# Expert products in float32r halves, and attention with scores one step ahead of the attended sums

## What is computed

```python
# attention, per sequence of 114 rows
xn = layernorm(h)
qk = silu(xn @ wqk + bqk);  q = qk*gamma[0]+beta[0];  k = qk*gamma[1]+beta[1]
v  = silu(xn @ wv + bv)
s  = q @ k.T / 114 + relative_bias          # causal
a  = laplacian(s)                           # (1 + erf(...)) / 2
h  = h + a @ v
# experts, per row: top 2 of 8
xn = layernorm(h)
w, e = softmax over the two largest of xn @ w_router.T
y  = sum_k w_k * ((silu(xn @ w_gate[e_k].T) * (xn @ w_up[e_k].T)) @ w_down[e_k].T)
out = h + layernorm(y) * ln_gamma + ln_beta
```

## Time and profile before

| | |
|---|---|
| runs | median 1163.66 us (1160.97 to 1164.1, 3 runs) |
| profiled execution | 1162.72 us, its span 1160.9 us |
| TensorE busy over the span | 1019.3 us (88%), mean granted clock 0.929 |
| VectorE, ScalarE, GpSimd busy | 714.1, 578.9, 601.2 us |
| chain that ended last, by engine | TensorE 71%, VectorE 7%, GpSimd 5%, DMA 5%, ScalarE 5% |

### The profile page before, as it was taken

How to read it: one execution, slowest core, us unless ns; L and a number is a source line. 1 busy time by engine, 2 the same in 40 slices (tenths; PEclk the granted TensorE clock), 3 DMA queues, 4 the chain that set the end, 5 groups by cost and what they waited for, 6 DMA issues and landing times.

```text
span 1160.9 us, 19799 instructions
## 1 busy us (share of the span) xinstructions
PE 1019.3 (88%) x5646; PEld 818.8 (71%) x5647; DVE 714.1 (62%) x1864; ACT 578.9 (50%) x1273; POOL 601.2 (52%) x662
## 2 busy tenths in 40 slices
PE   5888999999999999998898862999999999999920
PEld 3678999999999999997576641566666666666610
DVE  1666999999999998886666652233333333333337
ACT  1466777877787777664766740222222222222223
POOL 4533776677667767777356565133333333333346
PEclk8998999999999999998978865999999999999965
DMA  9460001000100000120475323122222222222263
GB/s 272 125 182 18 1 1 65 1 1 2 65 1 1 25 1 2 59 61 23 125 283 168 116 60 111 28 45 45 42 45 45 45 45 45 42 45 45 41 151 121
DMA packets 54733, 75.49 MB, mean 65 GB/s; under 512 B 9348, under 2 KB 46978, under 8 KB 52612
## 3 DMA queue, kind: packets, MB, share of 16 engines
q1 hardware_dynamic: 32680, 49.24, 13.5%
q0 software_dynamic: 16640, 18.53, 9.5%
q10 hardware_dynamic: 5340, 6.83, 2.1%
HBM read 45.38 MB, written 29.14 MB: 64 GB/s over the span
## 4 chain that ended last, share of the span: by engine, by line
PE 71%; DVE 7%; POOL 5%; DMA 5%; ACT 5%; issue 5%; SPq 2%; POOLq 0%; ACTq 0%; DVEq 0%
PE bank L1512 19%; PE bank L1224 15%; PE bank L1528 9%; PE bank L1289 7%; PE bank L1284 3%; PE bank L1520 2%; PE bank L1355 2%; PE bank L1367 2%; DMA xtok<-in_tok_emb,tokens_s 2%; PE bank L1272 2%; PE bank L1273 1%; SPq L515 1%; POOL xtok L1002 1%; PE bank L1503 1%; DVE arena_b L1684 1%
## 5 line engine op out<-in xcount | busy, mean ns | idle before, releaser
L1152 POOL DMA_INDIRECT yrows<-arena_b,dest_i x64 | 99.7, 1557 | 273.4 <-ACT arena_b L961 262.2
L1512 PE MATMUL bank<-arena_a,arena_b 128*128 x512 | 236.2, 604 | 0.8 <-ACT arena_b L949 0.6
L1684 DVE SCALAR_TENSOR_TENSOR arena_b<-bank,sml,arena_b 128x304 f32<-128x304 f32 (+2 forms) x384 | 195.3, 522 | 20.0 <-ACT arena_b L742 17.1
L1998 DVE TENSOR_TENSOR arena_b<-bank,arena_b 128x512 f32<-128x512 f32 x64 | 44.3, 692 | 203.0 <-PE bank L1512 203.0
L1512 PEld LDWEIGHTS bank<-arena_a,arena_b 128*128 128x128 f32 x512 | 93.2, 192 | 100.0 <-issue 99.8
L1224 PE MATMUL bank<-xt_hi,w_hi 128*128 128x308 f32 x512 | 159.6, 312 | 3.0 <-DVE arena_b L1684 1.7
L1224 PE MATMUL bank<-xt_hi,w_lo 128*128 128x308 f32 x512 | 156.9, 307 | 0.0
L1224 PE MATMUL bank<-xt_lo,w_hi 128*128 128x308 f32 x512 | 156.6, 306 | 0.0
L1034 POOL TENSOR_TENSOR y_lo<-arena_b,y_hi 128x308 fp32r<-128x308 f32 x128 | 108.9, 864 | 30.8 <-ACT y_hi L766 30.6
L1040 POOL TENSOR_TENSOR u_halves<-arena_b,u_halves 128x308 fp32r<-128x308 f32 x128 | 109.7, 864 | 28.9 <-ACT arena_b L754 28.8
L1528 PE MATMUL bank<-arena_a,arena_b 128*128 x512 | 121.6, 380 | 1.6 <-DVE arena_b L2014 0.9
(11 more groups left out here) (193 smaller groups left out, 2221.7 us busy)
## 6 DMA issues: line engine op xcount, KB each, us to landing
arena_b<-xrows SPq DMA_DIRECT2D x64, 129.5 KB, 2.1
arena_a<-in_w_gate SPq DMA_DIRECT2D x4, 1024.0 KB, 10.4
arena_a<-in_w_up SPq DMA_DIRECT2D x4, 1024.0 KB, 10.4
arena_a<-in_w_down SPq DMA_DIRECT2D x4, 1024.0 KB, 7.6
yrows<-arena_b SPq DMA_DIRECT2D x1, 3648.0 KB, 18.6
h_all<-seq SPq DMA_DIRECT2D x8, 448.0 KB
w_raw<-in_w_in SPq DMA_DIRECT2D x3, 1024.0 KB, 4.7
arena_a<-yrows SPq DMA_DIRECT2D x4, 448.0 KB
```

The lines of the kernel that those rows point to most:

```text
L1152: pool.indirect_dma_start(yrows, bass.IndirectOffsetOnAxis(ap=dest_i[:, k:k + 1], axis=0), f_y[k], None, compute_op=ALU.add).then_inc(y_se ...
L1512: mm = pe.matmul(bank[q][:, :], x_gt[k][:, d, :], w[:, d, bass.ds(e * FFN, FFN)], start=(d == 0), stop=(d == DC - 1))
L1684: dve.scalar_tensor_tensor(acc[:, :, back_:TXT], x[:, :, 0:TXT - back_], conv_w(s // GROUPS, c, tap), acc[:, :, back_:TXT], ALU.mult, ALU. ...
L1998: dve.tensor_tensor(f_h, bank[1][:, :], f_sg, ALU.mult).then_inc(f_hh, 1)
```

## The change

Two edits are made together. **Experts:** the weights of gate and the first half of the inputs of up are split once, after loading, into an upper half (`upper_weights`, ScalarE) and a remainder (`lower_weights`, VectorE), six pieces of 128 x 2048; three of each stand inside the last steps of attention, three behind it. The rows of a block are split too: `x_hi` and `x_raw` on ScalarE, `x_lo` (`lower_x`) on VectorE. Gate is then six fp32r matmuls, up three fp32r and one f32. `add_bias` moves from GpSimd to VectorE, destinations get four sets in place of two, the loops are unrolled by four, and `w_down` is loaded after attention into four separate places. The count of tiles per expert is rounded by arithmetic in place of a comparison and a sum. One pad row block replaces fifteen. **Attention:** the order of each `attn_step` is new, with `scores(g)` before `attended(g - 1)`, `gate_values(g, 0)` before the gelu and `gate_values(g, 1)` two steps of work ahead of its use; the silu table is loaded right behind the gelu.

```diff
 @block.sync
-                if k >= 2 and k % 2 == 0:
-                    sp.wait_ge(a_h2, k)
-                sp.dma_start(dst[:, c, cols], src[:, c, cols]).then_inc(ld_ffn, 16)
+                if k >= 2 and k % 2 == 0:
+                    sp.wait_ge(a_h2, k)
+                    sp.wait_ge(ld_ffn, 16 * k)
+                sp.dma_start(dst, src).then_inc(ld_ffn, 16)
...
+            sp.wait_ge(a_om, GROUPS * 2)
+            load_down(0)
+            load_down(1)
+            sp.wait_ge(m_lm, GROUPS)
+            load_down(3)
+            for k in range(2):
+                sp.wait_ge(x_sent[k], 16 * 2 * GB * (GROUPS // ROW_SETS))
+            load_down(2)
             sp.wait_ge(pad_ready, 2)
 @block.scalar
+            def upper_weights(k):
+                act.wait_ge(ld_ffn, 32 * (k // 2 + 1))
+                hi, _, raw = FFN_HALVES[k]
+                act.activation(hi, raw, ACT.Copy).then_inc(w_upper, 1)
...
+            def attn_step(g):
+                query_key_silu(g)
+                routed_turned(g - 2, 0); routed_turned(g - 2, 1)
+                query(g); key(g)
+                norm_rows(g + 1)
+                weight(g - 2)
+                gate_values(g, 0)
+                score_gelu(g)
+                rows_turned(g + 1, 0); rows_turned(g + 1, 1)
+                gate_values(g, 1)
+                if g - 1 == GROUPS - 1:
+                    for k in range(SPLIT_FIRST):      # 3
+                        upper_weights(k)
+                routed_norm(g - 1)
...
-                act.activation(x_gt[k], bank[2][:, 0:DC * P]...).then_inc(f_trc, 1)
+                act.activation(x_hi[:, k, :, :], bank[2][:, 0:DC * P]...).then_inc(f_trc, 1)
+                act.activation(x_raw[k], bank[2][:, P:DC * P], ACT.Copy).then_inc(f_raw, 1)
 @block.gpsimd
+            def attn_step(g):
+                send_rows(g - 3, 0, 5)
+                norm_ahead(g + 2)
+                routed_scale(g - 1)
+                send_rows(g - 3, 5, 8)
 @block.tensor
+            def attn_step(g):
+                query_key(g)
+                turn_routed(g - 2, 0); turn_routed(g - 2, 1)
+                ranks(g - 3)
+                values(g, 0)
+                router(g - 2)
+                scores(g)
+                attended(g - 1, 0); attended(g - 1, 1)
+                turn_rows(g + 1, 0); turn_rows(g + 1, 1)
+                values(g, 1)
+                bias_scores(g + 1)
...
-            pe.wait_ge(ld_ffn, 16 * len(FFN_PIECES))
+            pe.wait_ge(ld_ffn, 16 * (len(FFN_PIECES) + FC))
+            pe.wait_ge(w_lower, len(FFN_HALVES))
...
-                for q, w, sig, free in ((0, wg_s, f_gm, f_silu), (1, wu_s, f_um, f_hh)):
-                    wait(pe, free, j)
-                    for d in range(DC):
-                        mm = pe.matmul(bank[q][:, :], x_gt[k][:, d, :], w[:, d, bass.ds(e * FFN, FFN)], ...)
-                    mm.then_inc(sig, 1)
+                wait(pe, f_silu, j)
+                for d in range(DC):
+                    for w in (wg_hi, wg_lo):
+                        pe.matmul(bank[0][:, :], x_hi[:, k, d, :], w[:, d, cols], ...)
+                pe.wait_ge(f_low, j + 1)
+                for d in range(DC):
+                    mm = pe.matmul(bank[0][:, :], x_lo[:, k, d, :], wg_hi[:, d, cols], ...)
+                mm.then_inc(f_gm, 1)
+                wait(pe, f_hh, j)
+                pe.wait_ge(f_raw, j + 1)
+                for x, w in ((x_lo, wu_hi), (x_hi, wu_hi), (x_hi, wu_lo)):
+                    pe.matmul(bank[1][:, :], x[:, k, 0, :], w[:, cols], ...)
+                pe.matmul(bank[1][:, :], x_raw[k], wu_s[:, cols], start=False, stop=True).then_inc(f_um, 1)
 @block.vector
+            def lower_weights(k):
+                dve.wait_ge(w_upper, k + 1)
+                hi, lo, raw = FFN_HALVES[k]
+                dve.tensor_tensor(lo, raw, hi.bitcast(F32), ALU.subtract).then_inc(w_lower, 1)
...
+            def attn_step(g):
+                place_rows(g - 3)
+                norm_bias(g + 1)
+                norm_ahead_stats(g + 2)
+                if g - 2 == GROUPS - 1:
+                    for k in range(SPLIT_FIRST):
+                        lower_weights(k)
+                choose(g - 2)
+                scale_scores(g)
+                add_attended(g - 1, 0); add_attended(g - 1, 1)
+                routed_stats(g - 1)
+                count(g - 2)
+                routed_bias(g - 1)
+                invert(g)
+                weigh(g)
...
-            v2 = c.inc(dve.tensor_tensor(steps_b, cnt ... C_STEPS ..., ALU.is_gt))
-            v = c.inc(dve.tensor_reduce(ntile, steps_b, AX, ALU.add))
+            v2 = c.inc(dve.tensor_scalar(ntile, cnt, (P - 1) / 2, 1.0 / P, ALU.add, ALU.mult))
+            v = c.inc(dve.tensor_scalar(ntile, ntile, ROUND, -ROUND, ALU.add, ALU.add))
...
+            def lower_x(j, k):
+                dve.wait_ge(f_raw, j + 1)
+                wait(dve, f_um, j - 1)
+                dve.tensor_tensor(x_lo[:, k, :, :], bank[2][:, 0:DC * P]..., x_hi[:, k, :, :].bitcast(F32), ALU.subtract)
+            def expert_step(j, m, pair, last=False):
+                hidden(j, k)
+                lower_x(j + 1, 1 - k)
+                destinations(j, k, m)
+                hidden_turned(j, k)
+                if k == 1:
+                    add_bias(pair)
```

More of the change, by code:

```diff
@@ L324, in build @@
         EMBEDDED = 5
+        SPLIT_FIRST = 3
         BIAS_OPS = 3 * 3 + 11
-        LAST_LAG = 5
+        LAST_LAG = 3
+        SENT_FIRST = 5
         def pat_cols(i):
@@ L385, in build @@
         row_f = part(arena_b, BLOCKS)
-        at[0] = 0
+        assert at[0] <= SETS_AT
+        at[0] = 2 * WD_COLS
         x_g = [part(arena_b, ROW) for _ in range(2)]
-        x_gt = [part(arena_b, DC * P).rearrange("p (c t) -> p c t", c=DC) for _ in range(2)]
+        x_raw = [part(arena_b, P) for _ in range(2)]
+        final_at = at[0]
+        at[0] = SETS_AT + WD_COLS
         f_sg = part(arena_b, FFN)
@@ L401, in build @@
         y_rs = [part(arena_b, GB * 4, rows=SEQ).rearrange("p (s k) -> p s k", s=4) for _ in range(GROUPS)]
+        assert at[0] <= SETS_AT
+        at[0] = 0
+        y_rows = [part(y_all, GB * D, rows=SEQ).rearrange("p (k d) -> p k d", k=GB) for _ in range(GROUPS)]
+        y_n = [t[:, :, 0:D] for t in y_rows]
         bank = [ctx.enter_context(nc.psum_tensor(f"bank{k}", [P, 512], F32)) for k in range(8)]
@@ L1130, in _ @@
             pool.wait_ge(rows_kept, GROUPS)
-            def attn_step(i):
-                if has(i - 5):
-                    send_rows(i - 5, 6, 8)
-                if has(i):
-                    norm_ahead(i)
-                if i == 2:
-                    pool.memset(padbuf[:, :, :], 0.0).then_inc(pad_zero, 1)
-                if has(i - 4):
-                    send_rows(i - 4, 0, 6)
-                if has(i - 2):
-                    routed_scale(i - 2)
-            for i in range(2, GROUPS + LAST_LAG):
-                attn_step(i)
@@ L1148, in send @@
-            def send(j, k):
+            def attn_step(g):
+                if has(g - 3):
+                    send_rows(g - 3, 0, SENT_FIRST)
+                if has(g + 2):
+                    norm_ahead(g + 2)
+                if g == 0:
+                    pool.memset(padbuf[:, :], 0.0).then_inc(pad_zero, 1)
+                if has(g - 1):
+                    routed_scale(g - 1)
+                if has(g - 3):
+                    send_rows(g - 3, SENT_FIRST, 2 * GB)
+            for g in range(GROUPS + LAST_LAG):
+                attn_step(g)
@@ L1174, in _ @@
+            pool.wait_ge(blanked, 16)
+            for m in range(DEST_SETS):
+                send(m, m, 16 * ((m + 1) // 2))
+            with pool.Fori(1, BLOCKS // DEST_SETS) as four:
+                for m in range(DEST_SETS):
+                    send(four * DEST_SETS + m, m, four * (16 * DEST_SETS // 2) + 16 * ((m + 1) // 2))
             for g in range(GROUPS):
@@ L1991, in _ @@
             dve.wait_ge(tbl_ready, 2)
+            for k in range(SPLIT_FIRST, len(FFN_HALVES)):
+                lower_weights(k)
             def hidden(j, k):
@@ L2014, in hidden_turned, with add_bias @@
                 dve.tensor_copy(f_ht[k], bank[3][:, :].rearrange("p (c t) -> p c t", c=FC)).then_inc(f_htc, 1)
-            for j in range(2):
-                hidden(j, j)
-                destinations(j, j)
-                hidden_turned(j, j)
-            with dve.Fori(1, BLOCKS // 2) as pair:
-                for k in range(2):
-                    hidden(pair * 2 + k, k)
-                    destinations(pair * 2 + k, k)
-                    hidden_turned(pair * 2 + k, k)
+            def lower_x(j, k):
+                dve.wait_ge(f_raw, j + 1)
+                wait(dve, f_um, j - 1)
+                dve.tensor_tensor(x_lo[:, k, :, :], bank[2][:, 0:DC * P].rearrange("p (c t) -> p c t", c=DC),
+                                  x_hi[:, k, :, :].bitcast(F32), ALU.subtract).then_inc(f_low, 1)
+            def add_bias(b):
```

(18 more changed lines are left out.)

289 lines of the change are left out of this document (136 added, 153 removed).

## The result

The kernel after takes 1123.1 us (median of 4 runs, 1121.98 to 1125.7) against 1162.32 us for the kernel before on the same chip: ratio 0.967, interval 0.9639 to 0.9701. A later comparison of the same two kernels gave 0.9683 (0.9649 to 0.9716). The prediction was 1119. The profiled execution took 1125.7 us, the longest of the four, its span 1123.9 us, 37.0 us less than before.

| | predicted | measured |
|---|---|---|
| eighth attended sum begins | 669.5 us (−14.2) | 667.54 (−16.2) |
| from there to the first block transposes | 43.9 us (+4.8) | 47.86 (+8.8) |
| first block transposes to last down product | −35.2 us | 357.2 for 386.6 us, −29.4 |
| all of it | −44.6 | −36.8 (and −0.2 in the rest) |

A forecast was written before the change was run, and what follows sets the result against it. TensorE's order was taken to bound the experts, and waits such as `attended` on the values' silu attention. From 1162.72 us, experts -35.2 and attention with tail -9.4 gave 1118.1, forecast as a median of 1119, range 1107 to 1138.

The forecast's parts named there:

- The fp32r pass: Experts' gate and up: 0.226 us per 512-column pass, nine plus two f32 passes 2.89 us against 3.44.
- The rival of a slow pass: Experts: fp32r passes at 0.41 us instead, kernel 1225 us; slower stage from 0.287 us a pass; chance 0.04.
- The load loop: Experts: transposes, `x_hi`, `x_raw`, `lower_x`, `destinations` and load take 5.25 us, fitting the 5.37 us period by 0.1.
- the block loads come late: Experts, rival: period 5.55 to 5.75 us, gain only 0.17 to 0.37 us a block, kernel 1137 us; chance 0.13.
- Sum of the blocks: Experts: period 5.37 us instead of 5.92, 0.55 us saved a block, 35.2 us over 64 blocks.
- No wait in front of `attended`, a wait of 1 to 2 us in front of `turn_routed`: Attention, expected sign in the profile: the 2.2 us wait before the attended sums goes, TensorE idles before `turn_routed` instead.
- The loop over GpSimd: Attention: the loop from `place_rows` through sends, norms, `turn_routed` and `ranks` sets the step at 15.6 us.
- the rival gave the fall 16 in 100: Attention, rival to a full clock: half speed for 4 to 7 us a group, kernel 1134 us; chance 0.16.
- behind the query product and not behind the router: Attention: TensorE's 1.65 us idle per group would follow full-width products, so the full clock was expected to stay.
- The 6.7 us of first subtractions: Tail: three `lower_weights` on VectorE before the last group's `choose` lie beside sends; without these, some 3 us cost.
- I take 1.0: Tail: VectorE's 13.4 us of `lower_weights` lengthen row sends by 0 to 3.9 us, 1.0 taken.
- a send does not need the port throughout: Tail: neighbouring sends at 1.12 us were read against the rule that could hold up to 13.4 us of sends.

The follow-up runs named there:

- three sends first: Kernel after with three instead of five row sends ahead of the two norm steps on GpSimd: 1122.71 us, 0.9705 of the kernel before.
- attention alone: Kernel before with only the new attention step orders, expert products as before and no weight split: 1149.03 us, 0.9888 of the kernel before.
- destinations first: Kernel after with `destinations` ahead of `hidden` on VectorE, measured twice: 1122.49 us (0.9658 of the kernel before), then 1118.59 us (0.9631).
- upper halves in PSUM: Destinations first, plus ScalarE copying each upper weight half to PSUM banks, where VectorE's subtractions read it: 1113.21 us, 0.9593 of the kernel before.
- the kernels with and without the lock: Kernel after with SBUF-only weight subtractions, tail 44.8 us; variants include one subtracting a PSUM bank in four cuts, tail 40.3 us, 1117.46 us in all.

## Why the prediction came out as it did

By medians the forecast of 1119 is 4.1 us off. The profiled execution, 1125.7 us, is 7.6 us above the 1118.1 of the sum: 4 us of tail and 5.8 of blocks, less the 2 that attention gained beyond the forecast. That the median is nearer is luck, for the sum had no reason for it.

**The fp32r pass (right in kind, mis-sized).** "With the same surplus a 512-column pass is 0.226 us": removing one pass gives 14.8 / 64 = 0.231, and the chain 0.233. On top of that the first of the nine, which follows the hidden transposes, takes 0.32 instead of 0.23 us by its starts in the timeline (795.54 and 795.86). Gate and up cost 3.02 us, not 2.89. That is 0.13 us a block or 8.3 us, the largest miss. The size scaled from 308 columns was a little small, and the first pass had no term of its own. The rival of a slow pass, from 0.287 us on, was far off.

**The load loop.** "It fits, by 0.1 us" failed, though its times were about right. In one block `row_wt` ends at 816.94, SyncE issues the load at 817.81, the rows land at 819.85, and the transposes begin at 820.50: by "TensorE wants it at" the transposes they are early, by 0.65 us. What the sum left out is that the read of the expert's index for the down product stands behind the wait for the rows in TensorE's queue. Removing the lateness gives 5.8 to 6.5 us, 0.09 us a block. So the rival "the block loads come late" is there, but at a quarter to a half of the 0.18 to 0.38 us by which it lengthened the period (0.17 to 0.37 was the gain that it left). What delays the load is as named: `destinations` queued behind `hidden` and `lower_x`. That this costs the forecast's balance nothing is luck: the rest of the block, carried over from before at 2.48 us, is 2.39 without late loads, shorter by as much.

**Sum of the blocks.** 5.50 us instead of 5.37 is 8.3 us over 64 blocks, of which the blocks outside the period, mostly the first ones, give back 2.5 (386.6 − 64 x 5.92 = 7.7 us of them before, 357.2 − 64 x 5.50 = 5.2 after). The rest is the 5.8 us between −35.2 and −29.4.

**Attention.** "No wait in front of `attended`, a wait of 1 to 2 us in front of `turn_routed`" holds for the sums; in front of `turn_routed` it is 1.54 and 1.39 us in two steps and 0.65 in the other four, and another 0.73 stands in front of the query product. The loop over GpSimd, forecast at 15.6, is 15.2 us in the step where it binds: sends begin at 604.18 and 619.41. But in four of seven steps (14.15 to 14.48 us) a shorter loop sets the pace, through ScalarE. The chain of such a step:

```profile
640.13 1.09 issue
641.22 0.20 ACT warm L858
641.42 0.47 ACT arena_b L861
641.90 0.02 issue
641.92 1.28 ACT L862
...
643.75 0.53 ACT arena_b L842
...
644.66 2.07 ACT arena_b L878 x4
646.73 0.04 issue
646.77 1.00 PE bank L1417 x8
```

Gelu with its two table loads (the 1.28 us of L862 is one), the turned rows and the routing norm stand in line there. The run with three sends first agrees: its five inner steps are all 14.47 or 14.48 us, so with GpSimd's loop shortened this one is next. The steps are 0.64 us shorter in the mean than the 15.6 forecast, 4.5 us over seven; the first sum of this execution began 2.5 us later than that of the one before (562.80, 560.33), so the eighth is 2.0 us earlier than forecast.

**The clock.** Forecast as full; the rival gave the fall 16 in 100. Between the first sum and the idle of 4.02 us that ends at 660.90 (in it the clock falls to half and stays there until the blocks) it fell once, after the idle of 1.39 us in front of L1417 at 616.13, though full-width products had run before it:

```profile
618.00:622.00 4.00, 4.00 (x16) 3.19 (x15) 2.25 (x15) 3.04 (x6) 2.30 (x3) 0.57 0.24 68
...
622.00:658.00 36.00, 32.13 (x187) 24.41 (x186) 27.17 (x123) 27.09 (x50) 26.03 (x27) 1.00 0.25 66
```

The mean of 0.57 is mostly the half of 1.2 GHz. It made one step 16.9 in place of 15.2 us. The repeat of the same kernel had the same two idles (1.53 and 1.40 us) and no fall. Over the profiles with the new attention the clock fell after the first of these idles in three (attention alone and the first destinations first, with a step of 19.7 us; upper halves in PSUM, with one of 17.0), after the second in two (this one and the second destinations first), and in the rest after neither. The run with three sends first, whose idles are all 0.65 us at that place, has none. The reason given ("behind the query product and not behind the router") doesn't hold as a rule; what held is that most idles are shorter (0.65 to 1.5 us, 2.19 before). Why the same idle is followed by a fall in one execution and not in the next stays open, and with it 1.5 to 4.4 us of an execution's time.

**The tail.** The order's own 3.8 us was in the forecast (+3.8 without the sends' 1.0). The 6.7 us of first subtractions do lie beside sends, as said; VectorE's are over at 704.5, before the last send at 708.65. "I take 1.0" of held sends was the step that failed: six sends lost 5.1 us (2.27 + 1.89 + 1.90 + 1.92 + 1.90 + 1.90 less 6 x 1.12), and the kernels with and without the lock differ by 4.5 to 5.0. That is above the upper bound of 3.9, which I had scaled from one send of 1.52 us beside subtractions of 0.69 us. An instruction of 0.69 us can hold a send for no more than its own length; one of 2.28 can hold it three times as long. (A seventh send, of 1.44 us at 694.61, stands beside the table's instruction of 0.69 us, as the one of 1.52 did before the change.) And the neighbour at 1.12 us, which I read as "a send does not need the port throughout", had begun at 705.96, before the first such instruction (706.51).

## What to carry to other kernels

When TensorE's share of a period is cut, walk the load loop again, put first on its engine what lets the next transfer start, and look at what stands behind the wait for it in TensorE's queue: here half of the next cut was lost while the load was late, and in the kernel after TensorE was busy for 319.98 of 320 us all the same. A label of what ended an idle is a hint; whether it costs anything, the idle's length and an experiment tell. When an indirect send must run beside VectorE, look at where VectorE's operands lie and how long one instruction is, not at how busy it is: an operand in PSUM removed the delay, cuts of a quarter halved it, and an earlier place only moved it. A stall scaled from a short instruction is no bound for a long one.

## What was not expected of the hardware

A float32r matmul of 512 columns takes 0.23 us back to back, but 0.32 us as the first behind the f32 transposes. From the start of an index's read into a register to the weight load that uses it TensorE's queue takes 0.85 us, hidden only while the queue runs ahead. The clock can fall or stay in two executions of one kernel with the same idles. Two-input subtractions from SBUF were never lengthened themselves (2.28 to 2.29 us beside sends); only the sends stood. ScalarE copies 512 columns from SBUF to PSUM in 0.60 us and VectorE begins a subtraction of them every 0.60 us, so four cuts take 2.48 us from the first start to the last end where one whole instruction takes 2.29.
